# Last pass of a convolution and attention kernel: two image buffers of sixteen rows in place of four of eight

## The chip, the core and the metric

The kernel runs on one core of one Trainium2 chip. The metric is the device time of one execution in microseconds (us); the median of three runs is compared. A row marked with an engine's name is that engine's: PE is TensorE (matmul; PEld is its weight load), DVE is VectorE, ACT is ScalarE, POOL is GpSimd, SP is SyncE, which only issues transfers here. The core has 16 DMA engines that all transfers share.

## What is computed

The input x has 8 images of 512 channels of 128 by 128 float32 values. Layer 0 convolves pairs of channels down to 256 channels of 64 by 64, derives a gate for each channel from a clustering and a mixture model, scales, interpolates back to 128 by 128 and adds x. Layer 1 is an attention over a basis P of 64 cosine products; its result, too, is a product of a 64-row and a position matrix, scaled by gamma, and is added to the output of layer 0:

```python
up = jnp.repeat(gate[:, :, None, None] * x + x, 2, axis=1) * w_up[None, :, None, None]
x = _bilinear_up_x2(up) + sx                       # layer 0, sx is the input
...
out = jnp.einsum('bvk,bkn->bvn', WvxP, out / lamdv) + out_bias
return gamma * out.reshape(Bb, Cc, Hh, Ww) + x     # layer 1
```

So the last step, for every image, is: read the input image again, add the interpolated part, the attention part and a shift for each channel, write the output image. An image is 33.55 MB to read and 33.55 MB to write.

## The kernel before

`first_pass` reads x once, makes the small convolved images (`downsampled`, 4.19 MB for each of the 8 images) and projections. `gather_pass` and `mixture_pass` derive the gates. `second_pass` is the last pass, and the only function that changes. It begins at about 1180 us of 2621 us.

The last pass goes through an image in 32 units of 4 rows (HALF = 4, UNITS = 32). Two units are a chunk of 8 rows (ROWS2 = 8, CH2 = 16 chunks to an image). The 512 channels lie on 128 partitions in T = 2 halves t of S = 2 channels each. In one unit:

- ACT weighs rows of the small image (tile `dd`) into `mid` and `part` (L1341), two chunks ahead, and copies transposed tiles (L1362, L1365).
- DVE adds them (L1457), scales half of the left factors (L1024), and POOL scales the other half (L1024).
- PE transposes (L1209, L1222) and multiplies into four PSUM banks `o` (L1239), one bank n for each of the four channel sets.
- DVE adds bank n and the shift to the image in place (`add`, L1476): banks 0 and 1 belong to t = 0, banks 2 and 3 to t = 1. The first add of a buffer's half t waits for its load (semaphore `x_in[i][t]`).
- POOL issues the stores of a finished chunk, one for each t, 1 MB each (`store`, L1273), after its scaling work of the next unit. Landing raises `y_out[i][t]`.

SP issues the loads in a fixed order. After the set-up it brings the first chunks; then, in the step of each odd unit, it issues the two loads of the chunk three ahead (`load_image`, L1058, 1 MB each). A load into a buffer waits on SP until the store of the chunk that was in it has landed. In every fourth unit, ahead of the image loads, SP issues a load of 8 rows of the small image (`load_rows`, L1049, 512 KB, for three such blocks ahead), so this load also stands behind the waits of the image loads before it:

```python
if free and landed > 0:
    sp.wait_ge(y_out[i][t], landed * 16)
sp.dma_start(xt[i][:, t, :, :, :].rearrange("g s h w -> g s (h w)"),
             xv[b + m // CH2, t, :, :, m % CH2 * ROWS2 * W:(m % CH2 + 1) * ROWS2 * W]
             ).then_inc(x_in[i][t], 16)
```

A chunk of 8 rows of a channel is 1024 contiguous values in memory and in the buffer, so each packet of a load or a store is 4 KB; a load of one t is 256 packets, 16 on each DMA engine. Four buffers `x0` to `x3` of 16 KB a partition for each t pair hold the image chunks. While images follow each other, the steps of the next image's small attention products (`stage`) are spread over the units of the present one.

Of the kernel before, what the change touches and what calls it, by code (L numbers as in the profile page):

```python
# [11 lines left out]
B, C, H, W = 8, 512, 128, 128  # L12
P = 128
T, S = 2, 2
# [907 lines left out]
ROWS2 = 8  # L922
CH2 = H // ROWS2
# [5 lines left out]
HALF = ROWS2 // 2  # L929
UNITS = H // HALF  # L930
PAIRS = HALF // 2
BANKS = TS
XBUF = 4
AHEAD = XBUF - 1
FACTORS = UNITS - 3
SET_UP = 4

# [8 lines left out]
def second_pass(nc, x, cst, p_cols, att_cols, inter, wqk_sb, wv_sb, vx, gam, xd, xps, coef, out):  # L946

    xv = x.rearrange("b (t g s) h w -> b t g s (h w)", t=T, s=S)
    ov = out.rearrange("b (t g s) h w -> b t g s (h w)", t=T, s=S)
    with Scope(nc, "second") as sc:  # L950
        xt = [sc.sb(f"x{i}", [P, T, S, ROWS2, W]) for i in range(XBUF)]
        dd = sc.sb("dd", [P, T, DRING, WD])
        p_sb = sc.sb("p", [P, H, UV])

# [63 lines left out]
        def chunk_of(u):  # L1018
            return u // 2
# [20 lines left out]
        with nc.Block() as block:  # L1040
            @block.sync
            def _(sp):
                def load_rows(b, j):

                    slot, n = j % DSLOTS, j % LOADS

                    sp.wait_ge(weighted, b * CH2 + 2 * j - 5 + CHUNK_LEAD)
                    rows = xd[b + j // LOADS].rearrange("t g n -> g t n")
                    sp.dma_start(dd[:, :, slot * DLOAD:(slot + 1) * DLOAD, :].rearrange("g t h w -> g t (h w)"),  # L1049
                                 rows[:, :, n * DLOAD * WD:(n + 1) * DLOAD * WD]).then_inc(dd_in[slot], 16)  # L1050

                def load_image(b, m, t, free=True):
                    i = m % XBUF
                    landed = b * (CH2 // XBUF) + m // XBUF
                    if free and landed > 0:

                        sp.wait_ge(y_out[i][t], landed * 16)
                    sp.dma_start(xt[i][:, t, :, :, :].rearrange("g s h w -> g s (h w)"),  # L1058
                                 xv[b + m // CH2, t, :, :, m % CH2 * ROWS2 * W:(m % CH2 + 1) * ROWS2 * W]
                                 ).then_inc(x_in[i][t], 16)  # L1060

                def prologue():
                    sp.dma_start(att[:, :], att_cols).then_inc(att_in, 16)
                    for j in range(DSLOTS - 1):
                        load_rows(0, j)
                    sp.dma_start(p_sb[:, :, :], p_cols.rearrange("w (h k) -> w h k", k=UV)).then_inc(p_in, 16)
                    for m in range(AHEAD):
                        for t in range(T):
                            load_image(0, m, t, free=False)
                def step(b, u, more):  # L1070
                    m = chunk_of(u)
                    if u % 4 == 3 and (more or m // 2 + DSLOTS - 1 < LOADS):
                        load_rows(b, m // 2 + DSLOTS - 1)
                    for t in range(T):
                        if u % 2 == 1 and (more or m + AHEAD < CH2):
                            load_image(b, m + AHEAD, t)

                batches(sp, step, prologue)
                for i in range(XBUF):
                    for t in range(T):  # L1080
                        sp.wait_ge(y_out[i][t], B * CH2 // XBUF * 16)
# [182 lines left out]
            @block.gpsimd  # L1264
            def _(pool):
                start_free(pool, [left_made[1]])

                def store(b, m):

                    i = m % XBUF  # L1270
                    for t in range(T):
                        pool.wait_ge(added[t * S + S - 1], b * UNITS + 2 * m + 2 + FREE)
                        pool.dma_start(ov[b, t, :, :, m * ROWS2 * W:(m + 1) * ROWS2 * W],  # L1273
                                       xt[i][:, t, :, :, :].rearrange("g s h w -> g s (h w)")
                                       ).then_inc(y_out[i][t], 16)

                for b in range(B):
                    pool.wait_ge(coef_in, b + 1)
                    for u in range(UNITS):
                        pool.wait_ge(mid_copied, b * UNITS + u + 1 + FREE)  # L1280

                        pool.wait_ge(multiplied, (b * UNITS + u) * BANKS - BANKS + UNIT_LEAD)
                        scale_rows(nc.gpsimd, left_made[1], mid_copy, hi, 0, u)
                        if u % 2 == 0 and b + u > 0:
                            store(b if u else b - 1, (u // 2 - 1) % CH2)
                store(B - 1, CH2 - 1)
# [104 lines left out]
            def _(dve):  # L1391
# [76 lines left out]
                                            ALU.mult).then_inc(zt_made, 1)  # L1468

                def add(b, u, n):  # L1470
                    m, rows = chunk_of(u), slice(u % 2 * HALF, (u % 2 + 1) * HALF)
                    i = m % XBUF
                    if n % S == 0 and u % 2 == 0:
                        dve.wait_ge(x_in[i][n // S], (b * (CH2 // XBUF) + m // XBUF) * 16 + 16)
                    dve.wait_ge(multiplied, (b * UNITS + u) * BANKS + n + 1 + UNIT_LEAD)
                    nc.vector.scalar_tensor_tensor(out=xt[i][:, n // S, n % S, rows, :], in0=ob[n][:, :, :],  # L1476
                                                   scalar=shift[:, n:n + 1], in1=xt[i][:, n // S, n % S, rows, :],
# [200 lines left out]
```

## Time and profile before

| | us |
|---|---|
| median of 3 runs | 2627.66 (2626.4 to 2629.55) |
| the profiled execution, its own time | 2623.3 |
| its span, from the first to the last instruction | 2621.5 |
| PE, DVE, ACT, POOL busy in the span | 2318.4, 2144.2, 1185.6, 925.9 |
| image loads of the last pass | 256 of 1024 KB |
| image stores of the last pass | 256 of 1024 KB |

The profile is one execution. The last pass is its last 1440 us. Busy shares of the whole span mix stages with different limits, so what bounds the last pass has to be read from windows inside it.

### The profile page before, as it was taken

To read this page: it belongs to the slowest core of one execution; us is meant where nothing else is said; L and a number is where in the kernel's file an instruction comes from. 1 tells how busy PE (TensorE), PEld (TensorE's weight loads), DVE (VectorE), ACT (ScalarE), POOL (GpSimd) and SP (SyncE) were. 2 spreads that over 40 slices of the span, in tenths; PEclk is the share of its full clock that TensorE was granted. 3 is DMA by queue.
4 is the path that set the end of the run, shared out by engine and by line. 5 is a ranking of instruction groups with operands and counts; after the bars stand their busy time and mean duration, and the time that the engine had idled before them with its cause. 6 is when DMAs were issued, how large, how long until landed. Compare 5 with 4: busy or idle time off the path is not lost.

```text
span 2621.5 us, 51999 instructions
## 1 busy us (share of the span) xinstructions
PE 2318.4 (88%) x20691; PEld 1566.8 (60%) x20691; DVE 2144.2 (82%) x2312; ACT 1185.6 (45%) x3170; POOL 925.9 (35%) x644
## 2 busy tenths in 40 slices
PE   6999999999995775865998989899999998999887
PEld 2222222222221632434988988888888888888787
DVE  3889989989987425563998999889889998899897
ACT  0101001001000202324777777677777776777774
POOL 1211111112110000001665655556555555555554
PEclk9999999999997896996999999999999999999999
DMA  9999999999994725006999999999999999999998
GB/s 363 388 389 388 389 389 356 378 389 389 389 387 146 303 119 89 0 0 264 361 418 409 417 418 416 418 415 400 417 395 417 418 406 416 413 402 418 412 413 346
DMA packets 493922, 921.78 MB, mean 352 GB/s; under 512 B 211713, under 2 KB 212097, under 8 KB 491266
## 3 DMA queue, kind: packets, MB, share of 16 engines
q1 hardware_dynamic: 284802, 616.61, 61.0%
q0 software_dynamic: 69632, 268.45, 25.2%
q10 hardware_dynamic: 139264, 33.59, 5.8%
q8 instruction: 158, 2.59, 0.4%
q14 instruction: 66, 0.54, 0.1%
HBM read 615.00 MB, written 303.56 MB: 350 GB/s over the span
## 4 chain that ended last, share of the span: by engine, by line
DMA 21%; PE 20%; DVE 5%; ACT 4%; issue 3%; POOL 2%; SPq 0%; POOLq 0%; DVEq 0%; ACTq 0%
PE second_o L1239 14%; DMA second_dd<-downsampled 10%; DMA out<-second_x 8%; DMA second_x<-in_x 2%; PE second_mid_t L1209 2%; DVE second_x L1476 2%; POOL second_left L1024 2%; PE second_st L1099 1%; ACT second_mid L1341 1%; ACT second_left L1353 1%; DVE second_mid L1457 1%; DVE second_left L1024 1%; PE second_zt_t L1222 1%; ACT second_mid_copy L1362 1%; ACT second_part L1341 0%
## 5 line engine op out<-in xcount | busy, mean ns | idle before, releaser
L1239 PE MATMUL second_o<-second_right,second_left 128*128 128x128 f32 x8192 | 1074.9, 280 | 118.2 <-issue 44.4
L1239 PEld LDWEIGHTS second_o<-second_right,second_left 128*128 128x128 f32 x8192 | 991.0, 194 | 153.4 <-issue 143.1
L1024 POOL TENSOR_TENSOR second_left<-second_mid_copy,second_coef_rep 64x1024 f32<-64x1024 f32 x256 | 609.4, 2381 | 941.5 <-ACT second_mid_copy L1362 914.4
L1476 DVE SCALAR_TENSOR_TENSOR second_x<-second_o,second_shift,second_x 128x512 f32<-128x512 f32 x1024 | 727.7, 737 | 132.4 <-PE second_o L1239 119.9
L278 PE MATMUL first_conv<-first_x,first_band 64*64 64x512 f32 (+2 forms) x6144 | 548.6, 616 | 20.0 <-DMA first_x<-in_x 20.0
L252 ACT ACTIVATE first_staged<-first_conv 128x512 f32<-128x512 f32 x128 | 76.6, 598 | 739.7 <-issue 389.3
L278 PEld LDWEIGHTS first_conv<-first_x,first_band 64*64 64x64 f32 (+1 forms) x6144 | 166.4, 118 | 393.4 <-issue 383.4
L217 DVE TENSOR_TENSOR first_product<-first_freq,first_cols 128x4096 f32<-128x4096 f32 x64 | 283.2, 4425 | 124.0 <-PE first_freq L302 121.9
L202 POOL TENSOR_TENSOR first_band<-first_shift,first_w_all 128x576 f32<-128x576 f32 x128 | 145.6, 1159 | 647.2 <-PE first_conv L278 639.9
L1341 ACT ACTIVATE second_mid<-second_dd,all_inter 128x128 f32<-128x128 f32 x1024 | 313.8, 390 | 59.6 <-DMA second_dd<-downsampled 56.9
L1341 ACT ACTIVATE second_part<-second_dd,all_inter 128x128 f32<-128x128 f32 x1024 | 313.7, 390 | 3.2
L1024 DVE TENSOR_TENSOR second_left<-second_mid_t,second_coef_rep 64x1024 f32<-64x1024 f32 x256 | 308.8, 1206 | 1.1 <-PE second_mid_t L1209 0.6
L221 DVE TENSOR_REDUCE first_freq<-first_product 128x32 f32<-128x4096 f32 x64 | 282.9, 4420 | 2.2
L302 PE MATMUL first_freq<-first_x,first_rows 128*32 128x512 f32 x2048 | 232.6, 594 | 0.0
L1362 ACT ACTIVATE second_mid_copy<-second_mid_t 64x512 f32<-64x512 f32 x256 | 151.8, 593 | 152.7 <-PE second_mid_t L1209 150.0
L1273 POOL DMA_DIRECT2D out<-second_x x256 | 173.6, 681 | 98.8 <-DVE second_x L1476 40.5
L1209 PE MATMUL second_mid_t<-all_const,second_mid 128*128 128x128 f32 x1024 | 165.9, 286 | 19.1 <-DVE second_mid L1457 18.5
L1457 DVE TENSOR_TENSOR second_mid<-second_mid,second_part 128x1024 f32<-128x1024 f32 x128 | 173.5, 1356 | 3.5 <-ACT second_part L1341 3.5
L302 PEld LDWEIGHTS first_freq<-first_x,first_rows 128*32 128x32 f32 x2048 | 61.5, 110 | 167.5 <-issue 166.6
L1365 ACT ACTIVATE second_right<-second_zt_t 64x256 f32<-64x256 f32 x256 | 96.8, 378 | 121.9 <-PE second_zt_t L1222 121.1
L1209 PEld LDWEIGHTS second_mid_t<-all_const,second_mid 128*128 128x128 f32 x1024 | 119.6, 145 | 34.2 <-DVE second_mid L1457 26.7
L1222 PE MATMUL second_zt_t<-all_const,second_zt 128*128 128x128 f32 x512 | 98.9, 275 | 0.0
(231 smaller groups left out, 1460.8 us busy)
## 6 DMA issues: line engine op xcount, KB each, us to landing
first_x<-in_x SPq DMA_DIRECT2D x128, 2048.0 KB, 21.5
second_x<-in_x SPq DMA_DIRECT2D x256, 1024.0 KB, 19.3
out<-second_x POOLq DMA_DIRECT2D x256, 1024.0 KB, 10.8
downsampled<-first_staged ACTq DMA_DIRECT2D x512, 64.0 KB, 10.9
second_dd<-downsampled SPq DMA_DIRECT2D x64, 512.0 KB, 20.5
gather_two<-downsampled SPq DMA_DIRECT2D x4, 2048.0 KB, 14.7
gather_four<-downsampled SPq DMA_DIRECT2D x4, 2048.0 KB, 19.1
gather_raw<-downsampled SPq DMA_DIRECT2D x3, 2048.0 KB, 10.4
```

The costliest lines, as they stand in the source:

```text
L217: nc.vector.tensor_tensor(product[:, :, :, :], freq_ps[g % FREQ_BANKS][:, :, :].unsqueeze(2).broadcast_to(shape), cols[:, :, :].unsqueeze( ...
L221: nc.vector.tensor_reduce(freq[:, g, :, :], product[:, :, :, :], AX.X, ALU.add).then_inc(freq_summed, 1)
L278: made = nc.tensor.matmul(conv_ps[(2 * g + k) % CONV_BANKS][a * HD + place:a * HD + place + width * BLOCKS1, :, left:], band[tile % WEIGHT ...
L302: last = nc.tensor.matmul(bank[32 * q:32 * q + 32, :, :], rows[:, r, :], xt[(2 * g + a) % SLOTS1][:, half * HALF_B:(half + 1) * HALF_B, r, :],
L1024: return eng.tensor_tensor(left[a][rows, odd:HALF:2, :, :].rearrange("p n (t s) g -> p n t s g", t=T), turned[rows, :, :, :].unsqueeze(3). ...
L1209: last = nc.tensor.transpose(mid_t[:, n, t, :], mid[m % 2][:, t, r:r + 2, :].rearrange("p h w -> p (h w)"), k("ident"))
L1239: last = nc.tensor.matmul(ob[n][:, r, :], left[a][:, r, n, :], right[a][:, r, :], start=True, stop=True)
L1273: pool.dma_start(ov[b, t, :, :, m * ROWS2 * W:(m + 1) * ROWS2 * W], xt[i][:, t, :, :, :].rearrange("g s h w -> g s (h w)")).then_inc(y_out ...
L1341: last = nc.scalar.activation((mid[c], part)[r][:, :, 2 * i + 1 - e, :], dd[:, :, row(i + e + r - 1), :], ACT.Copy, scale=row_w[:, 2 * e + ...
L1362: nc.scalar.activation(mid_copy[hi, :, :, :], mid_t[hi, :, :, :], ACT.Copy).then_inc(mid_copied, 1)
L1457: nc.vector.tensor_tensor(mid[c][:, :, :, :], mid[c][:, :, :, :], part[:, :, :, :], ALU.add).then_inc(interpolated, 1)
L1476: nc.vector.scalar_tensor_tensor(out=xt[i][:, n // S, n % S, rows, :], in0=ob[n][:, :, :], scalar=shift[:, n:n + 1], in1=xt[i][:, n // S, ...
```

## The change

The four buffers of eight rows become two of sixteen rows; the memory is the same. A load brings sixteen rows of one t, 2 MB in packets of 8 KB, and there are 128 loads in place of 256. SP issues them in every fourth unit, for the buffer two ahead, and each waits until both stores (of the two chunks) of its half buffer have landed. Stores stay as they are, 8 rows in packets of 4 KB, now from one half of a buffer. The adds index the half of the buffer, and wait for a load once in four units.

```diff
-XBUF = 4
-AHEAD = XBUF - 1
+XBUF = 2
+D2 = CH2 // 2
...
-        xt = [sc.sb(f"x{i}", [P, T, S, ROWS2, W]) for i in range(XBUF)]
+        xt = [sc.sb(f"x{i}", [P, T, S, 2 * ROWS2, W]) for i in range(XBUF)]
...
                 def load_image(b, m, t, free=True):
                     i = m % XBUF
-                    landed = b * (CH2 // XBUF) + m // XBUF
+                    landed = b * (D2 // XBUF) + m // XBUF
                     if free and landed > 0:
-                        sp.wait_ge(y_out[i][t], landed * 16)
+                        sp.wait_ge(y_out[i][t], 2 * landed * 16)
                     sp.dma_start(xt[i][:, t, :, :, :].rearrange("g s h w -> g s (h w)"),
-                                 xv[b + m // CH2, t, :, :, m % CH2 * ROWS2 * W:(m % CH2 + 1) * ROWS2 * W]
+                                 xv[b + m // D2, t, :, :, m % D2 * 2 * ROWS2 * W:(m % D2 + 1) * 2 * ROWS2 * W]
                                  ).then_inc(x_in[i][t], 16)
...
-                    for m in range(AHEAD):
+                    for m in range(XBUF):
...
-                        if u % 2 == 1 and (more or m + AHEAD < CH2):
-                            load_image(b, m + AHEAD, t)
+                        if u % 4 == 3 and (more or m // 2 + XBUF < D2):
+                            load_image(b, m // 2 + XBUF, t)
...
                 def store(b, m):
-                    i = m % XBUF
+                    i, half = m // 2 % XBUF, slice(m % 2 * ROWS2, (m % 2 + 1) * ROWS2)
                     for t in range(T):
                         pool.wait_ge(added[t * S + S - 1], b * UNITS + 2 * m + 2 + FREE)
                         pool.dma_start(ov[b, t, :, :, m * ROWS2 * W:(m + 1) * ROWS2 * W],
-                                       xt[i][:, t, :, :, :].rearrange("g s h w -> g s (h w)")
+                                       xt[i][:, t, :, half, :].rearrange("g s h w -> g s (h w)")
                                        ).then_inc(y_out[i][t], 16)
...
                 def add(b, u, n):
-                    m, rows = chunk_of(u), slice(u % 2 * HALF, (u % 2 + 1) * HALF)
+                    m, rows = u // 4, slice(u % 4 * HALF, (u % 4 + 1) * HALF)
                     i = m % XBUF
-                    if n % S == 0 and u % 2 == 0:
-                        dve.wait_ge(x_in[i][n // S], (b * (CH2 // XBUF) + m // XBUF) * 16 + 16)
+                    if n % S == 0 and u % 4 == 0:
+                        dve.wait_ge(x_in[i][n // S], (b * (D2 // XBUF) + m // XBUF) * 16 + 16)
```

## Rows read from the trace of the kernel before

**Rows 1.** Windows: stretch, length us, busy us of each engine, PE's clock, DMA share, GB/s.

```profile
1240.00:1411.86 171.86, 158.12 (x1306) 148.98 (x1305) 157.00 (x204) 128.15 (x362) 96.88 (x64) 0.98 1.00 393
...
1411.86:2279.95 868.09, 793.76 (x6531) 745.26 (x6532) 790.96 (x1026) 645.40 (x1821) 487.53 (x321) 0.98 1.02 412
...
2288.00:2320.00 32.00, 30.48 (x262) 29.09 (x262) 31.74 (x40) 25.01 (x74) 19.42 (x13) 1.00 1.02 385
```

**Rows 2.** DMA view of 2000 to 2024 us: packets, then each queue's.

```profile
DMA packets 2722, 10.04 MB, mean 418 GB/s; under 512 B 151, under 2 KB 151, under 8 KB 2719
...
q0 software_dynamic: 1307, 5.06, 51.6%
q1 hardware_dynamic: 1412, 4.93, 50.5%
```

**Rows 3.** Waits of 1411.86 to 2279.95 us (five images): total, times, longest.

```profile
ACT second_mid L1341 <- DMA second_dd<-downsampled: 31.8, 14, 4.7
...
DVE second_x L1476 <- DMA second_x<-in_x: 3.4, 6, 1.0
```

**Rows 4.** Waits of SP's own queue, same five images.

```profile
SPq L1058 <- DMA out<-second_x: 748.3, 160, 8.9
```

**Rows 5.** The chain that ended last, 1984 to 2035 us: start, length us.

```profile
1987.69 13.05 DMA out<-second_x
...
2001.34 22.73 DMA second_dd<-downsampled
...
2024.40 2.14 ACT second_mid L1341 x7
...
2029.66 2.05 PE second_o L1239 x8
```

**Rows 6.** Timeline of DVE, 2285 to 2298 us: start, length us.

```profile
2285.65 0.75 DVE L1476 SCALAR_TENSOR_TENSOR second_x<-second_o,second_shift,second_x 128x512 f32<-128x512 f32 x1 [4.55 <-PE second_o L1239]
...
2287.45 1.39 DVE L1476 SCALAR_TENSOR_TENSOR second_x<-second_o,second_shift,second_x 128x512 f32<-128x512 f32 x2
...
2295.34 0.75 DVE L1476 SCALAR_TENSOR_TENSOR second_x<-second_o,second_shift,second_x 128x512 f32<-128x512 f32 x1 [0.15 <-PE second_o L1239]
```

**Rows 7.** Timeline of POOL, 2285 to 2300 us.

```profile
2294.17 0.68 POOL L1273 DMA_DIRECT2D out<-second_x  x1 [0.20 <-issue]
2295.49 0.68 POOL L1273 DMA_DIRECT2D out<-second_x  x1 [0.65 <-PE second_o L1239]
```

**Rows 8.** DMA view of 900 to 960 us (loads of `gather_pass`, 16 KB rows).

```profile
DMA packets 363, 5.16 MB, mean 86 GB/s; under 512 B 48, under 2 KB 48, under 8 KB 48
...
q1 hardware_dynamic: 361, 5.13, 20.0%
```

**Rows 9.** DMA view of 2001 to 2005 us, both queues full.

```profile
q0 software_dynamic: 213, 0.87, 53.0%
q1 hardware_dynamic: 213, 0.81, 49.3%
```

**Rows 10.** Stores (L1273) issued from 1600 to 2500 us, issue to landing.

```profile
DMA to landing us min/median/max: 8.9/11.5/15.1
```

**Rows 11.** The same for stores of 1230 to 1290 us.

```profile
DMA to landing us min/median/max: 4.4/8.3/12.6
```

**Rows 12.** Image loads (L1058) issued from 1600 to 2500 us.

```profile
DMA to landing us min/median/max: 11.1/19.3/23.9
```

**Rows 13.** Loads of the small image (L1049), whole span.

```profile
DMA to landing us min/median/max: 3.7/20.5/24.5
```

**Rows 14.** Timeline of 2575 to 2622 us: the last waits for a load.

```profile
2607.79 4.93 DVE L1476 SCALAR_TENSOR_TENSOR second_x<-second_o,second_shift,second_x 128x512 f32<-128x512 f32 x6 [0.63 <-DMA second_x<-in_x]
```

## The prediction, made before the changed kernel ran

> **What bounds the kernel now.** I cut the last pass into images with the windows, at the first matmul of the next image's products (L1099), which comes once an image. Five images take 868.09 us, 173.6 each, and move 412 GB/s [rows 1]; 412 x 868.09 / 5 gives 71.5 MB, the 67.1 MB of x and output and 4.2 MB of small image. Inside an image the DMA view shows both queues never empty and 418 GB/s [rows 2]. At that rate the bytes take 171 us. The rest, 2.5 us an image, is idle DMA around an image's start, where the rate falls to 385 for 32 us [rows 1]. So the transfers are the bound, closely.
>
> The engines are close behind. Waits that a DMA ends sum to 31.8 + 3.4 us in the five images [rows 3]; without them an image would take (868.1 - 35.2) / 5 = 166.6 us, 20.8 for each sixteen rows. The plain pace is 2295.34 - 2285.65 = 9.69 us for 8 rows [rows 6], 19.4 for 16; the other 1.4 are the next image's products.
>
> Third, what holds a transfer back. SP waits for stores in 748 of 868 us, always at L1058 [rows 4]: each load leaves the moment a store has landed. The chain that ended last goes store 13.05 us, small-image load 22.73, then ACT and PE [rows 5]. With four buffers, one goes round in four chunks, 4 x 10.85 = 43.4 us; in it lie compute with the issue of the last store, 9.84 (from 2285.65 to 2295.49, [rows 6, 7]), a second-half store, 13.05 [rows 5], and a load, 19.3 [rows 12]: 42.2. About one microsecond is spare.
>
> **The change, part by part.** First, the packets. The gather's loads show that long rows do go as single packets: 361 packets for 5.13 MB [rows 8]; without the 48 small ones, 20.0% of 16 engines x 60 us / 313 = 613 ns for 16 KB. A 4 KB packet takes 53.0% of 16 x 4 us / 213 = 159 ns [rows 9]. On the line between, 8 KB takes 159 + 454 / 3 = 310 ns against 318 for two. There are 65,536 load packets of 4 KB in the pass, 32,768 of 8 KB after: 32,768 x 8 / 16 = 16 us less DMA work, 2.1 an image. It shows in the time only while the queues stay full. Bounds for the saving: zero, if 8 KB costs like two packets, and 20 us, with 2 ns more a packet from the rounding of the shares.
>
> Second, instructions. SP issues 128 loads less; its queue waits 86% of the time, so this is worth nothing. DVE does the same adds with half the waits on a load; DVE's add is held by one for only 3.4 us now [rows 3], again nothing. The small-image load still leaves after the stores of the same chunk have landed, but with two or four megabytes ahead of it as before; it is needed after some 25 us, and that wait can only shrink when fewer loads stand in the queue.
>
> Third, the buffer's round, which is the matter. A buffer of 16 rows can't be refilled until its second half has been stored, and there is only one other buffer to work from. So two periods P are: compute, from the first add to the issue of the last store; that store's landing, S; the load's landing, L; less 2.4 us, since the second load is first needed at bank 2 (the add after 2287.45 starts about 2288.1, [rows 6]).
> - Compute = 9.69 + 9.84 + 1.4 = 20.9 [rows 6, 7].
> - S. Least 5.6: two stores of 1.05 MB at 418 GB/s take 5.0 and the shortest landing shows 4.4 - 2.5 = 1.9 beside its bytes [rows 11], less the 1.3 between the issues [rows 7]. Most 15.1 [rows 10]. In a full queue the least is 8.9 and the median 11.5, half of them first-half stores. After the change the loads of the other buffer have just ended, so part of it runs alone: I take 11.0.
> - L. The two loads are 4.19 MB, 9.9 us at 423 GB/s (8192 bytes in 310 ns on 16 engines), and 2.5 beside (3.7 less 1.25 for half a megabyte, [rows 13]); they leave 1.3 us apart, so least 9.9 + 2.5 - 1.3 = 11.1 from the second's issue. But the stores of the other buffer's first half are issued 8.5 and 9.84 us into its compute, just as these loads leave, and another 2.1 MB, 5.0 us, goes between: 16.1. These stores stand behind the tail of the earlier ones, so not all get ahead of the load's last packet: 14.6.
>
> The sum: 2P = 20.9 + 11.0 + 14.6 - 2.4 = 44.1, P = 22.05, an image 176.4 us against 173.6. That is above the transfers' floor, 171 - 2.1 = 169, and above the engines' 166.6, so the round is the new bound. One microsecond more in S + L makes 4 us an image.
>
> Over the pass: the first image runs its first two buffers from the set-up at the engines' pace, 2 x 20.8 + 6 x 22.05 = 173.9 against 171.9 [rows 1]: +2.0. Seven images at +2.8: +19.6. At the end, the last awaited load now covers 16 rows: from its landing 20.9 - 2.4 + 5.6 = 24 us remain, where now 2621.5 - 2607.8 = 13.7 do [rows 14]; as the last loads will have come with fewer others in the queue I count 4 of these 10. Total +25.6. On the profiled execution's 2623.3 us that gives 2649; it lies 4.4 below the median, and the difference carried over gives 2653.
>
> A rule that bears on L. At 2001 to 2005 us, with both queues full, each had 213 packets taken [rows 9]: turn and turn about, whatever their size. The Trainium skill, DMA: Bandwidth & Descriptors, section Queues, rings and completion order, says that each DMA engine takes turns between its queue rows packet by packet; the trace agrees, 213 to 213. By that rule a load's turn will carry twice a store's bytes; if turns went by bytes instead, L would be 16.1 in place of 14.6, S shorter by about as much, and the sum the same.
>
> **The rivals.**
> (A) The round is the bound, as above, +8 to +75 us: chance 0.58.
> (B) The transfers stay the bound. For: the floor of 169 is only 7 us under 176.4; S + L need be 1.9 us each shorter than taken to reach it. Then an image loses 2.1 us of packet time and keeps some idle: 171.5 to 173, and the pass is 5 to 16 us faster, 2612 to 2623 at the median. Against: no buffer is spare, so every latency shows. Chance 0.19. The same page, section Anatomy of one DMA, fits a fixed 2.0 us plus bytes at 436 GB/s to each DMA, 4.4 us for 1 MB; the least store here agrees, 4.4 [rows 11]. By it, 128 fewer loads save 128 x 2.0 us if they ran one by one; here the queue is full (102% share in [rows 1]), so only in (B) would any of it be seen.
> (C) Saving and loss cancel within 0.2% (5 us), which is also what a measurement of this kernel can tell from no change: 0.08. It includes that 8 KB goes as two packets and the round just fits.
> (D) Stores starve. With loads taking two bytes in three, a store beside them needs 2.1 x 3 / 0.42 = 15 us, and if loads and stores meet all the time S is 15.1 and L 16.1: 2P = 49.7, an image 199, +200 at the most. From S + L = 27.5 on, an image of 184, it is +75 and more. Against: stores and the other buffer's loads take their turns one after the other. Chance 0.15.
>
> **The numbers.** Likeliest is (A), 2653 us. Its own range is 2636 to 2700. For 8 in 10 I go down to 2614, into most of (B), and up to 2705, leaving about a tenth at each end. Slower by over 0.2%: 0.58 + 0.15 = 0.73; faster 0.19; within 0.2% 0.08.
>
> **What would show it.** In the changed kernel's profile: GB/s inside an image below 418, near 71.5 MB / 176.4 us = 405, with the DMA share under 1; the small-image wait of ACT (31.8 us) nearly gone, and in its place DVE waiting at L1476 for the image load, once per sixteen rows; stores landing 8 to 15 us; loads 12 to 15, well under 19.3. The chain that ended last alternates store and image load. Packet time of 8 KB: 310 ns. The prediction is wrong if images keep 171 to 173 us with 418 GB/s or more (then (B)), or if the store's landing is above 14 at the median (D).

## The result and the profile after

The changed kernel takes 2704.65 us at the median of four runs (2702.23 to 2705.78), the kernel before in the same comparison 2627.03 (2623.84 to 2629.55): ratio 1.0295, 95% interval 1.0277 to 1.0313. That is 77.6 us slower, where 25.6 were forecast. It is 0.35 us inside the upper end of the range (2705). Two of the five executions of the kernel that leaves out the stores of a first half, below, took 5892 and 6795 us and are left out of its median. The profiled execution has a span of 2702.9 us against 2621.5, so 81.4 to find.

The windows are cut like those of before, near the first L1099 matmul of the next image's products; columns as in [rows 1]. The first cut lies 0.3 us ahead of that matmul (1421.13) and the last 1.5 us behind it (2342.00), so the 184.5 us an image below are 184.2 by the matmuls themselves.

```profile
1240.00:1420.85 180.85, 161.07 (x1309) 151.28 (x1309) 157.71 (x205) 128.92 (x366) 97.61 (x65) 0.97 0.94 367
1420.85:2343.50 922.65, 805.47 (x6538) 755.21 (x6537) 793.29 (x1028) 646.18 (x1827) 489.14 (x322) 0.97 0.99 388
```

The first image costs 180.85 - 171.86 = 9.0 us more and the next five 54.6 more, 184.5 each in place of 173.6; the remaining 81.4 - 9.0 - 54.6 = 17.8 lie in the last two. Every image pays about the same 9 to 11 us. The rate fell from 412 to 388 GB/s and the DMA share from 1.02 to 0.99. An image needs 71.6 MB; 71.6 / 0.388 = 184.5.

The waits of four images (1605.36 to 2343.50 us): total, times, longest; then those of SP's own queue.

```profile
DVE second_x L1476 <- DMA second_x<-in_x: 55.3, 22, 5.1
```

```profile
SPq L1058 <- DMA out<-second_x: 697.0, 65, 19.8
```

ACT's wait for the small image, 31.8 us in [rows 3], is not in the list any more. DVE's wait for the image load has grown from 3.4 us in five images to 55.3 in four, 22 times in 32 periods of sixteen rows. SP's longest wait for a store is 19.8 us against 8.9 [rows 4].

The chain that ended last, over two rounds of one buffer, start and length:

```profile
2013.51 0.75 DVE second_x L1476
...
2030.40 14.05 DMA out<-second_x
2044.47 15.37 DMA second_x<-in_x
2059.86 0.31 DVE second_x L1476
...
2077.27 13.49 DMA out<-second_x
2090.78 16.24 DMA second_x<-in_x
```

It is the round that the prediction drew: adds from bank 2 on, the issue of the last store, its landing S, the load's landing L. But S + L is 29.4 and 29.7 us where 25.6 were taken, and the adds take 16.9 and 17.4 where 20.9 - 2.4 = 18.5 were. The rounds are 46.3 and 47.2 us; over five images 2P is 184.5 / 4 = 46.1, against 44.1 forecast.

Landings of stores (L1273) and of image loads (L1058) issued from 1600 to 2500 us, each from its own line's view:

```profile
DMA to landing us min/median/max: 5.8/13.0/18.4
```

```profile
DMA to landing us min/median/max: 8.1/12.7/17.4
```

The store's median rose from 11.5 [rows 10], the load's fell from 19.3 [rows 12]. The windows inside one period show where the transfer rate goes:

```profile
1980.00:1997.00 17.00, 16.42 (x144) 15.70 (x143) 16.85 (x21) 13.10 (x38) 9.82 (x6) 1.00 1.01 412
1997.00:2000.00 3.00, 2.71 (x25) 2.55 (x24) 3.00 (x5) 2.60 (x9) 2.15 (x3) 1.00 0.85 285
2000.00:2003.00 3.00, 3.00 (x29) 3.00 (x28) 3.00 (x4) 2.44 (x8) 2.63 (x2) 1.00 0.99 348
2003.00:2009.00 6.00, 5.84 (x51) 5.46 (x49) 6.00 (x9) 3.81 (x12) 2.31 (x1) 1.00 1.01 424
2009.00:2016.00 7.00, 6.14 (x51) 5.82 (x52) 6.32 (x9) 5.17 (x16) 3.77 (x4) 1.00 1.02 410
2016.00:2020.00 4.00, 4.00 (x35) 3.77 (x35) 4.00 (x7) 3.30 (x10) 2.99 (x2) 1.00 1.02 414
```

The queues are named in the DMA view: in 1997 to 2000 us the loads' queue holds 77.6% of the engines' time and the stores' queue 7.8%; in 2016 to 2020 us the stores' queue holds 100.3% and the loads' queue 0.4%.

```profile
q1 hardware_dynamic: 93, 0.76, 77.6%
q0 software_dynamic: 32, 0.09, 7.8%
```

```profile
q0 software_dynamic: 419, 1.63, 100.3%
q8 instruction: 1, 0.02, 1.4%
q1 hardware_dynamic: 5, 0.01, 0.4%
```

So the work of a period comes in a batch. The last stores run down, SP's wait ends, and the refill starts on queues with almost nothing else in them, at 285 and then 348 GB/s. Against 418 these six microseconds lose 3 x (418 - 285) / 418 + 3 x (418 - 348) / 418 = 1.5 us. A period's 71.6 / 8 = 8.95 MB take 21.4 us at 418 GB/s; with 1.5 more that is 22.9 of the 23.06 measured. This is one period, but the others look alike. Cut into 240 windows of 3 us, the stretch from 1600 to 2320 us has 61 below 370 GB/s in the changed kernel, one or more at nearly every refill. The kernel before has 13, and all but one of these lie 13 to 29 us behind a first L1099 matmul; in between both queues held work [rows 2].

The same can be read from what a megabyte costs. These are the load queue's rows of 1600 to 2500 us, packets, MB and share of the 16 engines, of the kernel before and then of the changed one:

```profile
q1 hardware_dynamic: 56220, 195.23, 54.4%
```

```profile
q1 hardware_dynamic: 31988, 184.35, 54.0%
```

0.544 x 900 / 195.23 = 2.51 us of all engines for a megabyte before, 0.540 x 900 / 184.35 = 2.64 after. (In the full stretch 2003 to 2009 us it is 0.654 x 6 / 1.65 = 2.38.) The stores' queue stayed at 2.45. An image was DMA work of 1.024 x 173.6 = 177.8 us (the queues' shares added up) and is 0.991 x 184.5 = 182.8: 5.0 us more work, not 2.1 less; the other 5.9 of the image's 10.9 are time in which the engines were not busy.

### The profile page after: what moved, and what is told of

It is laid out like the page before. It is cut to its first block, busy times and chain, and to the rows that moved or that the text cites. A ratio compares the mean times of both kernels' runs of the same rounds, so it can differ in the third digit from the quotient of the medians.

```text
span 2702.9 us, 51741 instructions
## 1 busy us (share of the span) xinstructions
PE 2333.1 (86%) x20691; PEld 1582.1 (59%) x20691; DVE 2145.3 (79%) x2312; ACT 1183.6 (44%) x3170; POOL 925.3 (34%) x644
## 4 chain that ended last, share of the span: by engine, by line
DMA 23%; PE 19%; DVE 7%; issue 3%; ACT 2%; POOL 2%; POOLq 0%; DVEq 0%
PE second_o L1239 13%; DMA second_x<-in_x 13%; DMA out<-second_x 10%; DVE second_x L1476 2%; PE second_mid_t L1209 2%; DVE second_mid L1457 2%; DVE second_left L1024 1%; POOL second_left L1024 1%; PE second_st L1099 1%; ACT second_left L1353 1%; PE second_zt_t L1222 1%; POOL out L1273 1%; ACT second_part L1341 1%; PE second_st L1121 1%; DVE second_zt L1466 0%
## 5 line engine op out<-in xcount | busy, mean ns | idle before, releaser
L1239 PE MATMUL second_o<-second_right,second_left 128*128 128x128 f32 x8192 | 1086.9, 282 | 85.0 <-issue 48.9
L1239 PEld LDWEIGHTS second_o<-second_right,second_left 128*128 128x128 f32 x8192 | 1005.5, 197 | 118.7 <-issue 105.9
L278 PEld LDWEIGHTS first_conv<-first_x,first_band 64*64 64x64 f32 (+1 forms) x6144 | 166.1, 118 | 394.5 <-issue 387.8
L1273 POOL DMA_DIRECT2D out<-second_x x256 | 172.7, 675 | 137.4 <-DVE second_x L1476 66.9
L302 PEld LDWEIGHTS first_freq<-first_x,first_rows 128*32 128x32 f32 x2048 | 61.5, 110 | 167.5 <-issue 166.6
## 6 DMA issues: line engine op xcount, KB each, us to landing
second_x<-in_x SPq DMA_DIRECT2D x128, 2048.0 KB, 13.4
second_dd<-downsampled SPq DMA_DIRECT2D x64, 512.0 KB, 18.5
```

What stands on the lines that cost most here:

```text
L278: made = nc.tensor.matmul(conv_ps[(2 * g + k) % CONV_BANKS][a * HD + place:a * HD + place + width * BLOCKS1, :, left:], band[tile % WEIGHT ...
L302: last = nc.tensor.matmul(bank[32 * q:32 * q + 32, :, :], rows[:, r, :], xt[(2 * g + a) % SLOTS1][:, half * HALF_B:(half + 1) * HALF_B, r, :],
L1239: last = nc.tensor.matmul(ob[n][:, r, :], left[a][:, r, n, :], right[a][:, r, :], start=True, stop=True)
```

## The experiments

Ratios are to the kernel before, timed beside each experiment on the same chip; it had a median of 2623.5 to 2624.6 us in all of them, and 2627.0 beside the changed kernel. Differences between two experiments are therefore good to a few microseconds only.

**Long packets or coarse wait?** The first experiment keeps the changed kernel's buffers and waits and gives it back its short packets:

```diff
-                    sp.dma_start(xt[i][:, t, :, :, :]...
+                    for n in range(2):
+                        sp.dma_start(xt[i][:, t, :, n * ROWS2:(n + 1) * ROWS2, :]...
...
-                        dve.wait_ge(x_in[i][n // S], (b * (D2 // XBUF) + m // XBUF) * 16 + 16)
+                        dve.wait_ge(x_in[i][n // S], (b * (D2 // XBUF) + m // XBUF) * 32 + 32)
```

> Two buffers of sixteen rows with the same waits as the changed kernel, but each load goes as two of eight rows, in packets of 4 KB. Theory R (the round of a buffer sets the time: a load can leave only when the last of four stores of its buffer has landed, and the DMA queues run dry once per sixteen rows): the time stays with the changed kernel, 2690 to 2725 us. Theory K (long packets are slow by themselves: in the changed kernel q1 has 54.0% of 16 engines in two images for packets that would need less): back to the kernel before, 2620 to 2640 us.

Measured 2727.25 us, ratio 1.0386 (1.0369 to 1.0403), 383 GB/s, 2 us above the range of the first theory and 87 above that of the second. The long packets are not what slows the kernel; they give 23 us back. The coarse waits alone cost about 100: SP's for two stores before a load, and DVE's for sixteen rows before an add. The two were not taken apart. DVE's wait and the load queue's row, 1600 to 2500 us:

```profile
DVE second_x L1477 <- DMA second_x<-in_x: 75.2, 21, 7.0
```

```profile
q1 hardware_dynamic: 52169, 180.67, 54.8%
```

A megabyte of loads costs 0.548 x 900 / 180.67 = 2.73 us here, against 2.64 with long packets.

**More buffers.** Room for them was made by keeping only 8 rows of the position factor p, which leaves every compute instruction its size, and changes the values of the output. First the control with four short buffers, then six, then three of sixteen rows:

```diff
-XBUF = 4
+XBUF = 6      # or 3, with rows as in the change
-        p_sb = sc.sb("p", [P, H, UV])
+        p_sb = sc.sb("p", [P, ROWS2, UV])
```

> Control for the next two: the kernel before (four buffers of eight rows), but the tile p holds only its first eight rows, which are used for every chunk, so that 30 KB a partition come free; this leaves out loading and using the other rows of p, and the buffers are counted through all images. Both theories: the time of before, 2615 to 2630 us; at most some us less because 4 MB are not loaded at the start.

> Six buffers of eight rows, with the small tile p as in the control. Packets stay at 4 KB. Both theories: one microsecond was spare in the round of four; with six the transfers alone are the bound, an image 171 us or a little less than 173.6: 2600 to 2625 us.

> Three buffers of sixteen rows, same memory as the six of eight, loads of sixteen rows in 8 KB packets, small tile p. Theory R: with one more buffer the queues stay full, 8 KB packets take 310 ns, and the time is that of six buffers of eight less up to 16 us: 2590 to 2615 us. Theory K: 8 KB packets take about 346 ns also in a full queue, 36 ns x 32768 / 16 = 74 us more DMA work: 2670 to 2700 us.

Measured: four short 2624.82 (1.0003, 0.9993 to 1.0012), six short 2626.5 (1.0006, 0.9996 to 1.0015), three long 2613.85 (0.9952, 0.9936 to 0.9969), within the first theory's range. Six short buffers brought nothing, a miss: the kernel before wants no more buffers. With six, ACT still waits 35.8 us for the small image (39.5 before, both in 1600 to 2500 us), and the rate is 410 GB/s against 412. So the kernel before was bound by its transfers, as the prediction had it, and the step from a buffer round with nothing to spare to one with much to spare was worth nothing. With a third long buffer, and so half more memory for images, the change pays.

The same three buffers with short packets separate the two once more:

> Three buffers of sixteen rows and small tile p, waits as coarse as in the changed kernel, but loads of eight rows in 4 KB packets. If the coarse wait costs nothing once a third buffer keeps the queues full, and the whole 10.6 us that three long buffers gain over the kernel before is the packets': 2622 to 2630 us. If the third buffer itself gains, under 2620 us.

Measured 2647.5 (1.0095, 1.0078 to 1.0112), a miss by 20 us. Its load queue, and that of the three long buffers with long packets:

```profile
q1 hardware_dynamic: 55298, 191.65, 54.6%
```

```profile
q1 hardware_dynamic: 33828, 194.68, 53.2%
```

2.56 us for a megabyte with short packets and 2.46 with long ones. The last pass loads some 302 MB, so the difference of 0.105 us is 32 us, and 33.6 were measured between the two kernels (37 by their ratios). With two buffers it is 2.73 - 2.64 = 0.095, 29 us, and 23 were measured. So even with a third buffer the coarse wait costs 23 us if packets are short; long packets are worth 23 to 34 us under a coarse wait.

**Fewer short buffers.**

```diff
-XBUF = 4
+XBUF = 3      # or 2
```

> The kernel before with three buffers of eight rows instead of four (24 rows of memory instead of the changed kernel's 32). The round: three chunks = 10.5 compute with the issue of the last store, + S + L. If it is memory that is short in the changed kernel, this is slower than it, over 2705 us. If it is the grain (a load waits for sixteen rows to be stored, and the queues run dry), then with S 10 and L 13 the round is 33.5, 11.2 us a chunk against 10.85, and never dry: 2630 to 2680 us, faster than the changed kernel with a quarter less memory.

> The kernel before with two buffers of eight rows (16 rows of memory). Each refill waits for its one store, with one other buffer to work from, as in the changed kernel but twice as often. Theory D with the same gap per refill (1.7 us per eight rows beside 10.7 us of transfers): an image 16 x 12.4 = 198 us, 2790 to 2860 us in all. If the gap grows with the load's size, 0.9 us per eight rows: an image 185 us, about 2710 us.

Measured 2647.57 for three (1.0084, 1.0057 to 1.0111) and 2857.61 for two (1.0895, 1.0878 to 1.0912), both as expected. Three buffers of eight rows lose 23 us; the changed kernel has a third more memory for images and loses 78, so it is not memory that is short.

While a 16-row buffer is worked on and its last stores are prepared, 19.3 to 19.8 of its 46.1 us pass (the chain's 16.9 and 17.4 and the 2.4 up to bank 2), 42%; for an 8-row buffer before it is 9.84 of 43.4, 23%. What is left of the round for transfers fell from 77% to 58%. This share does not order the kernels by itself: two short buffers keep 61% (9.84 of 2 x 12.7 us) and lose three times as much as the changed kernel. The loss counted for each refill does. Two short buffers take (173.6 + 233.0 / 8) / 16 = 12.67 us for eight rows, whose bytes take 10.71 at 418 GB/s: 2.0 us lost. Two long buffers with the same 4 KB packets take (173.6 + 102.8 / 8) / 8 = 23.31 us for sixteen rows, whose bytes take 21.41: 1.9 us lost. So with two buffers a refill costs much the same whether it brings eight rows or sixteen, and the longer buffers halve the number of refills.

**The two terms of the sum, bare.** Here the stores of a buffer's first half are left out, and with them half the output:

```diff
-                        sp.wait_ge(y_out[i][t], 2 * landed * 16)
+                        sp.wait_ge(y_out[i][t], landed * 16)
-                        if u % 2 == 0 and b + u > 0:
+                        if u % 4 == 0 and b + u > 0:
```

> The changed kernel without the stores of each buffer's first eight rows: half of the output isn't written. It measures the two disputed landings by themselves. The prediction had put a lone last store at 5.6 us at the least and a pair of loads with nothing beside it at 11.1 us from the second's issue. If my terms were right for their bare parts, the landings fall to about 6 and 11 us, two periods of sixteen rows are 20.9 + 6 + 11 - 2.4 = 36 us, below the engines' 41.6, and the pass is bound by the engines: an image 167 us, 2560 to 2580 us in all. If the landings were too small also without the stores (a slow start of the queues), they stay at 8 and 13 or more; 39.5 is still under the engines' 41.6.

Measured 2563.92 us (0.9763, 0.974 to 0.9785), as expected. The trace is of a further execution:

> Once more the changed kernel without the stores of each buffer's first eight rows, for a profile of an execution of the usual length. Expected: 2560 to 2570 us, the last store's landing 5 to 7 us, the loads' 9 to 12 us, no wait of DVE for an image load.

2563.84 us, and for the issues of 1600 to 2500 us, with KB each and the median to landing:

```profile
second_x<-in_x SPq DMA_DIRECT2D x86, 2048.0 KB, 9.9
out<-second_x POOLq DMA_DIRECT2D x88, 1024.0 KB, 6.0
```

DVE no longer waits for a load at all. The prediction's least values, 11.1 for L and 5.6 for S, lie within about a microsecond of these medians (the least landings are 7.5 and 4.4). The excess is all in what it added for company in the queues. An image takes 173.6 - (2624.25 - 2563.92) / 8 = 166.1 us here, the engines' pace that the prediction gave as 166.6.

**The order of the stores.** Three kernels tried to bring the last stores home sooner. One stores 12 rows early and 4 late, one lets SP issue each buffer's last stores in the loads' own queue, and the third lets SP issue all stores, with the small image's load moved ahead by two units:

```diff
-                        pool.wait_ge(added[t * S + S - 1], b * UNITS + 2 * m + 2 + FREE)
+                        pool.wait_ge(added[t * S + S - 1], b * UNITS + 4 * m + (4 if last else 3) + FREE)
```

```diff
+                def store(b, m):     # now on SP, ahead of the loads
...
+                        sp.wait_ge(added[t * S + S - 1], b * UNITS + 2 * m + 2 + FREE)
+                        sp.dma_start(ov[...], xt[i][:, t, :, half, :]...).then_inc(y_last[i][t], 16)
```

> The changed kernel, but of each sixteen rows the first twelve are stored after the third unit and the last four after the fourth (packets of 6 KB and of 2 KB). The bytes are the same. Theory R1 (the last store stands behind the first-half store, which crawls beside the load at one byte in three): the load now runs alone for longer and the last store is small, so the round shortens by 1 to 2 us in 23: 2630 to 2680 us. Theory R2 (all that counts is that the queues run dry between the last store's landing and the next load's first packets, once per sixteen rows): no change, 2695 to 2715 us.

> The changed kernel, but the last store of each sixteen rows (its second eight) is issued by SP in the queue of the loads, just ahead of the loads that wait for it; the first-half stores stay in POOL's queue. Theory R in its form 'what the last store stands behind': it no longer stands behind the first-half store in POOL's queue, so its landing falls from 13 us to 8 to 9 us, what is left of the first-half store fills the queue while the next load starts, and two periods go from 46.1 to about 42, near the transfers' own 21.1 a period: 2605 to 2650 us. Theory D, 'the queues must run dry once per sixteen rows whatever the order': over 2685 us.

> The changed kernel with all stores issued by SP in the queue of the loads; POOL issues none. Everything goes through one queue in order: load, first-half store, small image, last store, and then the next load only when that store has landed, with nothing else queued. A first-half store no longer shares its time with a load. Theory D (dry queue): 8.9 MB at 420 GB/s, 21.3 us, and a gap of 1.5 us or more per sixteen rows, as in the changed kernel: 2680 to 2720 us. If instead sharing with the loads was the cost, it falls with it: 2610 to 2650 us.

Measured 2790.04 for the uneven stores (1.0624, 1.0604 to 1.0645), 2713.58 for the last stores on SP (1.0341, 1.0326 to 1.0355), 2747.28 for all on SP (1.0467, 1.0451 to 1.0483). All are slower than the changed kernel, and the first and third outside what either theory allowed. So "the last store stands behind other stores" falls: in the second the last stores landed after 11.7 us at the median and the loads after 13.4, and the kernel gained nothing. SP issues in a fixed order, though, and its queue now waited 361 of 900 us for the adds (none of that before), so this kernel changed more than the order of the stores. In the uneven kernel the windows show even less overlap:

```profile
2024.00:2028.00 4.00, 3.72 (x33) 3.46 (x32) 4.00 (x6) 3.44 (x11) 2.55 (x3) 1.00 1.03 426
2028.00:2030.00 2.00, 2.00 (x21) 2.00 (x19) 2.00 (x4) 1.44 (x5) 2.00 (x2) 1.00 0.91 227
2030.00:2036.00 6.00, 5.53 (x51) 5.14 (x50) 5.64 (x8) 5.07 (x16) 4.66 (x4) 1.00 1.02 414
```

From 2028 to 2030 us its loads' queue alone held work, 193 packets of 0.45 MB, mostly the small image: 227 GB/s.

**Staggering.** If stops between batches are the loss, shifting the buffers of t = 1 by eight rows against those of t = 0 should spread them:

```diff
+        def place(c, t):
+            return (c + t) // 2, (c + t) % 2
...
+                    t, g = (0 if u % 4 == 3 else 1), b * D2 + u // 4 + XBUF
+                    if u % 2 == 1 and chunks_in(g, t):
+                        load_image(g, t)
```

> The changed kernel with the buffers of the second channel half shifted by eight rows: its loads leave in the middle of a sixteen-row period, those of the first half at its end (at an image's edge the second half's load is two of eight rows). Memory, the wait for two stores per load, and 8 KB packets stay (15 of 16 loads). Theory D (both queues run dry once per sixteen rows, about 1.7 us of a period of 23.1): one half's stores and loads fill the other's gap, full rate inside an image, 8 KB packets save up to 16 us: 2605 to 2635 us. Theory G (a load that has to wait for two stores is late by itself, whatever else is queued): as the changed kernel, 2690 to 2710 us.

Measured 2698.43 (1.0286, 1.0269 to 1.0303), hardly better than the change and within what the rival theory G allowed, not D. But a new wait had appeared, since the small-image load now stood behind one more wait on SP (1600 to 2500 us):

```profile
ACT second_mid L1355 <- DMA second_dd<-downsampled: 74.4, 23, 6.3
DVE second_x L1491 <- DMA second_x<-in_x: 35.3, 22, 3.9
```

So ACT was made to issue the small image's loads itself (`load_rows` moved to ACT's program), with the shift and, as its control, without it:

> The staggered buffers, and the small image loaded by ACT in its own queue, which took 6 us off the kernel before and 14 us off three long buffers. Theory D: 6 to 14 us under e13_staggered, 2595 to 2620 us, faster than the kernel before. Theory G: 2685 to 2710 us.

> The changed kernel, unshifted, with the small image loaded by ACT in its own queue. If the shift of the buffers did nothing and ACT's queue did all in e14 (2676 us), this has 2670 to 2680 us too. If the shift helped once the small image was out of SP's order (theory D), this stays at 2695 to 2710 us, since ACT hardly waits for the small image in the changed kernel.

Measured 2675.8 with the shift (1.0173, 1.0147 to 1.0198) and 2715.19 without (1.0349, 1.0332 to 1.0366). Neither shifted kernel came out where D had it, the one with ACT's loads lies between the two theories (its executions range from 2660 to 2678 us), and the control is 5 us above its upper range. The shift is worth 1.8%, about half of the loss, but not the 70 us and more that were expected of it. The other half stays. The trace of the shifted kernel with ACT's loads shows that the stretches at a low rate did not go: 43 of its 240 windows of 3 us from 1600 to 2320 us are below 370 GB/s, against 64 in the control, and some are lower than any in the changed kernel:

```profile
2242.00:2245.00 3.00, 3.00 (x28) 2.90 (x27) 3.00 (x6) 1.94 (x6) 1.21 (x1) 1.00 0.57 231
2245.00:2248.00 3.00, 2.71 (x24) 2.55 (x24) 3.00 (x5) 2.58 (x9) 1.95 (x3) 1.00 0.60 190
```

The expectation that one half's transfers fill the other's gap was wrong; the gaps became fewer and deeper. Over the kernels the count rises with the time: 12 for three long buffers, 13 before, 32 for three short, 43 here, 61 for the change, 75 with its short packets, 110 for two short.

**A version that beats both.** ACT's own loads of the small image were first put into the kernel before, then with three long buffers (8 rows of p); last, the whole computation in that form. Room for the third buffer comes from storing p as its two cosine factors; DVE scales the row factor once an image and multiplies by the column factor for each chunk:

```diff
-                    nc.vector.tensor_tensor(zt[c][:, :, :], p_sb[:, rows, :],
-                                            rr[:, rows].unsqueeze(2).broadcast_to([P, ROWS2, UV]),
+                    nc.vector.tensor_tensor(zt[c][:, :, :].rearrange("p h (u v) -> p h u v", v=LOW),
+                                            dh_rr[:, rows, :].unsqueeze(3).broadcast_to(shape),
+                                            k("dw8").unsqueeze(1).unsqueeze(2).broadcast_to(shape),
                                             ALU.mult).then_inc(zt_made, 1)
```

> The kernel before, but the loads of the small image are issued by ACT in its own queue instead of by SP, behind no image load and behind no wait for a store. With six buffers the time did not fall and ACT still waited for these loads, so theory R for the kernel before says that they, not the buffers, bring the stalls within an image: their landing falls from 20 us to under 12 us, ACT's wait for them disappears. If the transfers alone bind (418 GB/s in a full queue), an image goes from 173.6 to 171 to 172 us, 2600 to 2615 us in all. The rival: the stall only changes its name (DVE waits for the image load), 2620 to 2630 us.

> Three buffers of sixteen rows with 8 KB load packets and the small tile p, and the small image loaded by ACT in a queue of its own. With three long buffers the time was 2613.9, and ACT still waited 42.6 us for the small image in 900 us; ACT's own queue took 6 us off the kernel before. If the two add up: 2600 to 2610 us; if the queue is full anyway, 2610 to 2616 us.

> Three buffers of sixteen rows with 8 KB load packets and the whole computation: the tile p (32 KB a partition) is replaced by its two factors (the product over rows is formed once an image, 1024 elements on DVE, the other factor comes in with the multiplication that is there anyway), two small tiles lie in constants that are no longer used, and the small image is loaded by ACT. With the small tile p this was 2599.7 us; one operation of about 1.2 us an image more on DVE: 2598 to 2612 us, faster than the kernel before.

Measured 2618.17 (0.9975, 0.9965 to 0.9985), 2599.68 (0.991, 0.9897 to 0.9924) and 2600.55 (0.9913, 0.9896 to 0.9929). The first falls between its two expectations: ACT's wait went, and DVE waited for the image loads in its place (40.7 us in 1600 to 2500). The second is 0.3 us below its range, the third inside it. The last computes everything that the reference asks and is 23 us faster than the kernel before and 104 faster than the changed one (100 by the ratios). It keeps three buffers of sixteen rows, half more memory for images than either. In 1600 to 2500 us it moves 416 GB/s, and no engine waits for a transfer but for

```profile
DVE second_x L1491 <- DMA second_x<-in_x: 3.9, 4, 1.6
```

## Why the prediction was right in direction and short in size

| step or term | forecast | shown |
|---|---|---|
| transfers bind before | yes, closely | yes: six buffers bring nothing |
| engines' pace, an image | 166.6 | 166.1 |
| four short buffers just suffice | 1 us spare | yes: three lose 23 us, six gain nothing |
| 8 KB packets | -2.1 us an image | 2% less per MB in a full queue; image's DMA work +5.0 all the same |
| small-image wait | shrinks | gone |
| buffer's round is the bound | 2P = 44.1 | yes, 46.1 |
| S, L bare | 5.6, 11.1 | 6.0, 9.9 at the median |
| compute, less 2.4 | 18.5 | 16.9 and 17.4 in the chain |
| S, L in company | 11.0, 14.6 | 14.05, 15.37 and 13.49, 16.24 in the chain |
| first image | +2.0 | +9.0 |
| the other images | +2.8 each | +10.9 each |
| end | +4 | -4 to -2, by the cut |

**What bounds now** held. The four short buffers that could be one fewer at 23 us, and the six that gain nothing, put the kernel before at the foot of both limits, as its rows did.

**The packets.** The forecast 310 ns against 318 is 2.5%. Under a full queue it held: 2.46 us for a megabyte with three long buffers against 2.51 before, 2%, with the small image's packets in both. What failed is the condition that stood beside it, "it shows only while the queues stay full", followed no further. In the changed kernel the queues don't stay full, and the load packets became 5% dearer, not 2.5% cheaper.

**The instructions and the small image** held: nothing on SP or DVE, and ACT's wait left the list.

**The round** is the step that failed, in its terms S and L. S = 11.0 was taken low in its bounds (5.6 to 15.1) because "the loads of the other buffer have just ended, so part of it runs alone". They had not ended. The last store of the chain is issued at 2030.40 us, and from 2030 to 2036 us the loads' queue still holds 61.2% of the engines' time; from 2036 to 2041 it brings the small image, which the sum for S leaves out (220 packets, 0.42 MB):

```profile
q1 hardware_dynamic: 237, 1.49, 61.2%
```

```profile
q1 hardware_dynamic: 220, 0.42, 21.7%
```

S is 14.05 and 13.49 where it is on the chain, and L is 15.37 and 16.24 and not 14.6. Their sum is 4.0 us larger, less the 1.3 us by which the adds took less, an error the other way that hid a third of it: 2.6 a round in these two, 2.0 on the mean. The prediction's own price, "one microsecond more in S + L makes 4 us an image", turns 2.0 into 8.0, and 2.8 + 8.0 is the 10.8 measured. The error was to add up two landings as if each met its own few companions. All stores and loads of a period share the same engines, and a batch that waits for the whole buffer starts on drained queues, with 1.5 us of each period lost below the full rate. A sum from the period fits better here: its bytes at the full rate, plus what each restart loses, 22.9 of 23.06 us. The loss of a restart was read from the changed kernel, though, and no row of before gives it; the 1.5 to 2.0 us are a measurement, not a forecast.

**The end** was forecast at +4. The last two images cost 17.8 together, less than twice 10.9, so it gave 4 back (2 by the matmuls: 19.3 and 10.6). The cause of that is open.

**The rivals.** (B), the transfers stay the bound, and (C) are out. (D) took S to 15.1 and L to 16.1; the store's median of 13.0 stays under the 14 that was its sign, but the measured +77.6 us is past its border of +75 and past (A)'s own range of 2636 to 2700. (The border is itself too low: by the prediction's sum S + L = 27.5 gives 7.7 + 7 x 10.4 + 4 = 85 us.) (A) and (D) differ in size only, and the result lies at their seam. That it still falls below 2705 is luck: that end was set to leave a tenth of the chances outside, not by a bound of S + L. The signs named for (A) came: a DMA share under 1, DVE's wait for the image load in place of ACT's for the small image, loads at 12.7 us and stores at 13.0, though 388 GB/s where 405 were named. The turns of the Trainium skill, DMA: Bandwidth & Descriptors, section Queues, rings and completion order, fit the full stretch: from 2003 to 2009 us the two queues had 218 and 217 packets taken, and the loads' 1.65 MB were nearly two bytes in three. The fixed 2.0 us of the section Anatomy of one DMA, given there for transfers that GpSimd issues, was not seen in 128 of SP's loads fewer: with three long buffers, joining each pair of loads gave 33.6 us, of which the packets' own time explains 32.

**What stays open.** Of what the coarse waits cost (some 100 us with two buffers), the first packets of a refill and the idle time are located in the trace; the part due to the stop of both halves t at once is half of it at most, by the shift. How it divides between SP's wait for two stores and DVE's for sixteen rows was not tested. Why all stores in SP's queue cost 1.7% more than the change, and why the uneven stores overlap so little, was not taken apart. That load packets in a drained queue take longer is measured (0.776 x 3 / 0.76 = 3.06 us for a megabyte from 1997 to 2000 us, 2.38 from 2003 to 2009); the cause inside the memory system is not.

## What to carry to other kernels

A buffer is busy while it is worked on, and what is left of its round is all that transfers have; halving the number of buffers at the same memory took that share from 77% to 58% here and cost 4%, of which longer packets gave back 1%. Coarsen transfers only with a buffer to spare: three of sixteen rows, with half more memory, are 0.5% faster where two are 3% slower. With two buffers count the refills: each cost 1.5 to 2.0 us beside its bytes, of eight rows as of sixteen. In a loop near its transfer bound a landing meets all that the period has in flight, and landing times added up with a few companions come out short.

## What the runs showed of the hardware that was not expected

- A refill on drained queues moved 285 GB/s in its first 3 us and 348 in the next 3, in the period shown, where full queues move 418 to 424.
- With two buffers and 4 KB packets a refill lost 2.0 us for eight rows and 1.9 for sixteen, so the loss goes by the refill and not by its bytes.
- The time that a megabyte of loads takes of the DMA engines is not a constant of the packet's size. With 4 KB packets it was 2.51 us in the kernel before, 2.56 with three coarse buffers and 2.73 with two; with 8 KB packets 2.46 and 2.64. Stores stayed at 2.45.
- Letting ACT issue the small image's loads, in a queue of its own and behind none of SP's waits, is worth 6 us to the kernel before and 11 to 14 to the one with three long buffers, and costs 11 to 14 with two. The queue and the order of issue were not taken apart.
